# Attention scores and row maxima of a fused transformer layer as pairs of 64-row TensorE tiles

## The reference, cut to what matters

```python
B, T, D, H, dh = 2, 2048, 256, 16, 16
q, k, v = split(x @ qkv_w + qkv_b)                       # per head (B, H, T, 16)
std_logits = einsum('bhqd,bhkd->bhqk', q, k) * dh ** -0.5
write_lines = exterior(x_prev @ w1_write, x @ w2_write)  # per head 6 numbers, unit length
read_lines = exterior(x @ w1_read, x @ w2_read)
geo_logits = einsum('bqhi,bkhi->bhqk', read_lines, write_lines @ J6) * inc_scale
std_out = softmax(causal(std_logits)) @ v
geo_out = softmax(causal(geo_logits)) @ (x @ geo_w + geo_b)
combined = (1 - gate) * std_out + gate * geo_out         # gate: mean sigmoid per token
x = layernorm(x + combined @ out_w + out_b)
x = layernorm(x + ffn(x))                                # silu(x wg) * (x wu) @ wd
```

## Time and profile before

| what | value |
|---|---|
| median of 3 runs | 2105.75 us (2104.53 to 2110.35) |
| profiled execution, first to last instruction | 2112.1 us |
| TensorE busy | 1930.6 us, 91% |
| ScalarE busy | 1273.4 us, 60% |
| VectorE busy | 1129.4 us, 53% |
| GpSimd busy | 336.9 us, 16% |
| mean granted TensorE clock | 0.962 |

### The profile page before, as it was taken

How to read it: one execution, slowest core, us unless ns; L and a number is a source line. 1 busy time by engine, 2 the same in 40 slices (tenths; PEclk the granted TensorE clock), 3 DMA queues, 4 the chain that set the end, 5 groups by cost and what they waited for, 6 DMA issues and landing times. The chain is left out here.

```text
span 2112.1 us, 35917 instructions
## 1 busy us (share of the span) xinstructions
PE 1930.6 (91%) x11400; PEld 769.0 (36%) x11400; DVE 1129.4 (53%) x2179; ACT 1273.4 (60%) x1641; POOL 336.9 (16%) x609
## 2 busy tenths in 40 slices
PE   8888498999998999999899999989999995899998
PEld 4444122333332333333233333323333322556555
DVE  5666377565564655556465655646565403443442
ACT  4555544577776777677677767767777783222121
POOL 3333303111211110111111011111101111000000
PEclk9999699999999999999999999999999997999999
DMA  6668660404133250414324041432500004112000
GB/s 192 205 211 254 163 107 25 86 21 90 37 70 46 50 86 6 91 20 73 49 47 86 6 91 21 72 46 50 86 6 30 4 11 103 43 51 65 20 20 20
DMA packets 138525, 145.83 MB, mean 69 GB/s; under 512 B 46784, under 2 KB 120768, under 8 KB 136288
## 3 DMA queue, kind: packets, MB, share of 16 engines
q1 hardware_dynamic: 137136, 140.32, 30.4%
q0 software_dynamic: 624, 2.75, 0.4%
q10 hardware_dynamic: 576, 0.28, 0.1%
HBM read 88.25 MB, written 54.53 MB: 68 GB/s over the span
## 5 line engine op out<-in xcount | busy, mean ns | idle before, releaser
L931 ACT ACTIVATE prob<-ex 128x1024 f32<-128x1024 f32 (+2 forms) x1280 | 1074.5, 893 | 444.4 <-PE ex L776 438.8
L946 DVE TENSOR_REDUCE mp<-mx 128x1 f32<-128x512 f32 (+3 forms) x1280 | 749.2, 609 | 547.4 <-PE mx L794 287.5
L776 PE MATMUL ex<-qa,ka 98*128 98x512 bf16 (+3 forms) x2560 | 675.6, 354 | 62.7 <-issue 28.3
L827 PE MATMUL pv<-prob,va 128*32 128x512 f32 (+3 forms) x5120 | 613.4, 552 | 7.6 <-POOL prob L752 7.3
L791 PE MATMUL mx<-ka,qa 96*128 96x512 bf16 (+3 forms) x1280 | 450.1, 353 | 14.7 <-DVE mp L946 13.8
L752 POOL TENSOR_SCALAR_AFFINE_SELECT prob<-prob 128x256 f32<-128x256 f32 x512 | 205.8, 408 | 1288.3 <-ACT prob L931 1287.8
L776 PEld LDWEIGHTS ex<-qa,ka 98*128 98x128 bf16 x2560 | 200.2, 99 | 474.3 <-ACT prob L931 306.3
L791 PEld LDWEIGHTS mx<-ka,qa 96*128 96x128 bf16 x1280 | 123.7, 97 | 340.4 <-DVE mp L946 239.1
L827 PEld LDWEIGHTS pv<-prob,va 128*32 128x32 f32 x5120 | 101.7, 108 | 206.7 <-issue 181.8
L1291 ACT ACTIVATE sg<-pg 128x512 f32<-128x512 f32 x48 | 28.7, 597 | 185.6 <-PE pg L1213 185.5
L794 PE MATMUL mx<-mask_qk,ident 128*128 128x128 bf16 x512 | 113.1, 221 | 0.0
(11 more groups left out here) (101 smaller groups left out, 964.7 us busy)
## 6 DMA issues: line engine op xcount, KB each, us to landing
parts<-sp SPq DMA_DIRECT2D x64, 384.0 KB, 3.3
qa<-parts SPq DMA_DIRECT2D x192, 128.0 KB, 6.7
ka<-parts SPq DMA_DIRECT2D x192, 128.0 KB, 8.6
values<-vn SPq DMA_DIRECT2D x64, 256.0 KB, 3.3
va<-values SPq DMA_DIRECT2D x16, 1024.0 KB, 13.8
heads<-on SPq DMA_DIRECT2D x64, 128.0 KB, 1.9
att<-heads SPq DMA_DIRECT2D x64, 128.0 KB, 3.0
xc<-in_xt SPq DMA_DIRECT2D x8, 513.0 KB, 4.2
```

Of the source, the lines that this page charges most:

```text
L776: last = pe.matmul(dst, ka[which][0:NROWM, h, kb * P:(kb + 1) * P], qa[which][0:NROWM, h, (qt + 1) * CH - w:(qt + 1) * CH], start=True, st ...
L827: last = pe.matmul(pv[h * VW:(h + 1) * VW, qt % 2, CH - w:CH], va[kind][:, kb, h * VW:(h + 1) * VW], prob[(s * HG + h) % 8][:, at[j]:at[j] ...
L931: act.activation(prob[n % 8][:, 0:w], ex[:, n % 2, 0:w], ACT.Exp).then_inc(ex_done, 1)
L946: v.tensor_reduce(out=mp[kind][:, h * NKB + qb, k0 // CH:k0 // CH + 1], in_=mx[:, u % 2, 0:w], axis=AX.X, op=ALU.max).then_inc(mx_free[kin ...
```

## The change

- The geometric numbers are no longer padded: 6 per head. In the projection they fill 2 row tiles of 96 rows and not 4 of 128, so NR is 6, and `t32` and `d32` have a buffer for each row tile. DRAM parts are two tensors now.
- A geometric score is 6 x 6 + 2 = 38 rows. Two heads lie in one operand, at rows 0 and 64, and the two matmuls use the two 64-row halves of the array. A dot-product score keeps 98 rows (odd heads: 128, with zeroed rows between).
- A unit of a step is now two heads and one block of keys, not one head and two blocks. The exponent still reads 1024 columns in a full step, and there are still four units in a step. `times_v` of block 0 waits only for the first two units.
- The maxima use 4 of the 6 products, 64 rows, and two heads at once in the two halves; a tile is a pair of heads, 80 tiles for each group of heads, and it takes both PSUM slots, so tile u waits for tile u - 1.
- The mask matmul is gone. VectorE masks instead: an off-diagonal pair is one reduce over 2 x 512 columns, a pair on the diagonal is two `tensor_tensor_reduce` instructions that add the mask and take the maximum, with their output thrown away into `dull`.
- `spread` weighs a geometric step 1.9 times a dot-product step. It gives the DOT item 28 pair tiles (15 off, 13 on the diagonal) and the GEO item 52 (33 and 19); the first item has 80 (48 and 32). There are four places in a step: before the first scores, before `times_v` of block 0, after it, and before `times_v` of block 1.
- The two maximum rows are copied by four DMAs, not two, and GpSimd sets rows of ones and zeros for each of the two operand sets in four memsets, in the first two items.

```diff
@@ load_operands
+    n = (NCOMP, DH)[kind]
     for i in which:
-        j, side, n = i // (2 * NCOMP), (i // NCOMP) % 2, i % NCOMP
-        src = parts[side, kind, b, (Q_PARTS, K_PARTS)[side][n], bass.ds(g * (HG * DH) + j * 2 * DH, 2 * DH), :]
-        q.dma_start((q_set, k_set)[side][n * DH:(n + 1) * DH, 2 * j:2 * j + 2, :],
-                    src.rearrange("(h d) t -> d h t", h=2)).then_inc(loaded[j], 16)
+        j, a, side, piece = i // 12, (i // 6) % 2, (i // 3) % 2, i % 3
+        to = (q_set, k_set)[side]
...
+        q.dma_start(to[row:row + 2 * n, at, :], src).then_inc(loaded[j], 16)
@@ project: first_rest
-                if not (head and m < 4):
-
-                    v.wait_ge(p3_done, c * NR + m - 3)
-                v.tensor_tensor(out=d32[m % 4][:, :], in0=t32[m % 4][:, :], in1=sp3[m][:, 0, :],
+                if not head:
+
+                    v.wait_ge(p3_done, (c - 1) * NR + m + 1)
+                n = ROWS[m]
+                v.tensor_tensor(out=d32[m][0:n, :], in0=t32[m][0:n, :], in1=sp3[m][0:n, SLOTS[m][0], :],
                                 op=ALU.subtract).then_inc(d_done, 1)
@@ attend: gpsimd, aside
+                if it < 2:
+                    i = it + 1
+                    done = 3 + it * 4
+
+                    g.wait_ge(masked, (it * len(DIAGONAL) + len(DIAGONAL) - TT // 2) * UNITS)
+                    g.memset(ka[i][96:98, 0:2, :], 1.0).then_inc(ones_ready, 1)
+                    g.wait_ge(ones_ready, done + 1)
+                    g.memset(ka[i][32:64, 2:4, :], 0.0).then_inc(ones_ready, 1)
...
@@ attend: tensor, scores
-                for (kb, w), c0 in zip(blocks, at):
-                    dst = ex[:, slot, c0:c0 + w]
-                    last = pe.matmul(dst, ka[which][0:NROWM, h, kb * P:(kb + 1) * P],
-                                     qa[which][0:NROWM, h, (qt + 1) * CH - w:(qt + 1) * CH],
+                kb, w = blocks[u // 2]
+                for a in range(2):
+                    dst = ex[:, pair, a * CH:a * CH + w]
+                    if kind == GEO:
+                        rows, at = slice(HALF * a, HALF * a + GEO_FULL), pair
+                    else:
+                        rows, at = slice(0, DOT_FULL[a]), 2 * a + pair
+                    last = pe.matmul(dst, ka[which][rows, at, kb * P:(kb + 1) * P],
+                                     qa[which][rows, at, (qt + 1) * CH - w:(qt + 1) * CH],
                                      start=True, stop=True)
@@ attend: tensor, max_tile
-                if u >= 2:
-
-                    pe.wait_ge(mx_free[kind], p * (NMX * COUNT[kind]) + (u - 1) * COUNT[kind])
-                dst = mx[:, u % 2, 0:w]
-                last = pe.matmul(dst, qa[which][0:NROW, h, qb * P:(qb + 1) * P],
-                                 ka[which][0:NROW, h, k0:k0 + w], start=True, stop=not on_diagonal)
-                if on_diagonal:
-                    last = pe.matmul(dst[:, w - P:w], ident16[:, :], mask_qk[:, :], start=False, stop=True)
+                if u >= 1:
+
+                    pe.wait_ge(mx_free[kind], p * (NMX * COUNT[kind]) + u * COUNT[kind])
+                for a in range(2):
+                    n = GEO_ROWS if kind == GEO else DOT_MAIN
+                    rows, at = slice(HALF * a, HALF * a + n), pair if kind == GEO else 2 * a + pair
+                    last = pe.matmul(mx[:, a, 0:w], qa[which][rows, at, qb * P:(qb + 1) * P],
+                                     ka[which][rows, at, k0:k0 + w], start=True, stop=True)
@@ attend: vector, max_tile
-                v.tensor_reduce(out=mp[kind][:, h * NKB + qb, k0 // CH:k0 // CH + 1], in_=mx[:, u % 2, 0:w],
-                                axis=AX.X, op=ALU.max).then_inc(mx_free[kind], COUNT[kind])
+                if on_diagonal:
+                    v.sem_inc(v_passed, 1)
+                    for a in range(2):
+                        last = v.tensor_tensor_reduce(out=dull[:, a, 0:w], in0=mx[:, a, 0:w], in1=mask_qk[:, CH - w:CH],
+                                                      scale=1.0, scalar=3 * MASKED, op0=ALU.add, op1=ALU.max,
+                                                      accum_out=to[:, a:a + 1])
+                else:
+                    last = v.tensor_reduce(out=to, in_=mx[:, :, 0:w], axis=AX.X, op=ALU.max)
+                last.then_inc(mx_free[kind], COUNT[kind])
@@ attend: tensor, step
-                scores(it, which, s, 0, head)
                 some(0)
-                scores(it, which, s, 1, head)
+                scores(it, kind, which, s, 0, head)
+                scores(it, kind, which, s, 1, head)
                 some(1)
                 if has_before:
                     times_v(*before, 0, head)
                 some(2)
-                scores(it, which, s, 2, head)
+                scores(it, kind, which, s, 2, head)
+                scores(it, kind, which, s, 3, head)
                 some(3)
-                scores(it, which, s, 3, head)
-                some(4)
                 if has_before:
                     times_v(*before, 1, head)
-                some(5)
```

More of the change, by code:

```diff
@@ L80 @@
 LAST_OF = {qt: max(s for s, x in enumerate(STEPS) if x[0] == qt) for qt in range(NQT)}
[L83 to L87, removed]
 def max_tiles():
     out = []
-    for h in range(HG):
+    for pair in range(HG // 2):
         for qb in range(NKB):
@@ L96, in max_tiles @@
             for k0 in range(0, end, CH):
-                out.append((h, qb, k0, min(CH, end - k0), k0 + CH >= end))
+                out.append((pair, qb, k0, min(CH, end - k0), k0 + CH >= end))
     return out
@@ L104, with spread @@
 MT_STEP = NSTEP - 2
-def spread(steps_of):
-    size = [sum(w for _, w in STEPS[s][1]) + 2 * P if s >= 0 else 0 for s in steps_of]
-    cols = [w + (P if d else 0) for _, _, _, w, d in MAXT]
+def spread(room):
+    cost = [(2 * w + 300) if d else (2 * w + 150) for _, _, _, w, d in MAXT]
     out, u, done = [], 0, 0
-    for i in range(len(steps_of)):
+    for i in range(len(room)):
         mine = []
-        while u < NMT and done + cols[u] / 2 <= sum(cols) * sum(size[:i + 1]) / sum(size):
+        while u < NMT and done + cost[u] / 2 <= sum(cost) * sum(room[:i + 1]) / sum(room):
             mine.append(u)
-            done += cols[u]
+            done += cost[u]
             u += 1
@@ L564, in chunk @@
                 v.wait_ge(dve, base + 7)
[L565 to L568 removed]
+                if not head:
                     v.wait_ge(rows_ready, c * NR)
                 v.tensor_tensor(
[L572 removed]
+                    out=ln[:, :, 1, :, :], in0=line_v[:, :, 0, :, :],
                     in1=rn[:, :, 0, :].unsqueeze(3).to_broadcast([P, TT, H, NCOMP]),
@@ L585, in _, with attend @@
                 first_rest(NC - 1, m, False)
-def attend(nc, parts, values, heads, ident, ident16, mask_qk, wide, out_w, out_b, wg, wu, wd, weights,
-           first):
+def attend(nc, parts, values, heads, ident, mask_qk, wide, out_w, out_b, wg, wu, wd, weights, first):
     with ExitStack() as ctx:
@@ L764, in _, with scores @@
             is_wide = pe.value_load(wide[0:1, 0:1], min_val=0, max_val=1)
-            def scores(it, which, s, h, head):
-                n = s * HG + h
-                slot = n % 2
+            def scores(it, kind, which, s, u, head):
+                n = s * UNITS + u
+                pair = u % 2
                 if not (head and n < 2):
@@ L848, in step @@
                 later = list(maxima[s])
-                where = [WHERE[min(len(later), 6)].count(i) for i in range(6)]
-                where[5] += max(len(later) - 6, 0)
+                where = [WHERE[min(len(later), 4)].count(i) for i in range(4)]
+                where[3] += max(len(later) - 4, 0)
                 def some(i):
```

212 lines of the change are left out of this document (124 added, 88 removed).

## The result

The changed kernel is slower: 2338.92 us median of 4 runs (2337.09 to 2344.12) against 2108.05 us for the kernel before on the same chip, a ratio of 1.110 (95% interval 1.108 to 1.112). The forecast was 2048 us, with a range up to 2120. Medians are of fast executions; the one run that was slow, 2331.91 us in the last experiment, is left out. The profiled execution agrees: its span is 2338.1 us against 2112.1.

What follows compares the result with a forecast made beforehand. TensorE was taken to bound the attention, with ScalarE next, and VectorE to pace the projection. Projection -24, seven head groups -40 and first item +6 sum to -58, from 2105.75 to 2048 us; range 1990 to 2120.

Steps and rivals of the forecast that it cites:

- costed at nothing: Work assumed hidden: GpSimd's memsets, SyncE's wait for them, four row copies, and 24 load issues an item ahead; no added time.
- The projection, -24: Projection: VectorE's chain starts 3.07 us earlier in each of 7 chunks, -21.5, and less GpSimd work at the end, -2.9.
- the low end: Projection: if the shorter wait keeps TensorE's clock up, up to 1.6 us more a chunk, -11.
- A dot-product item, 84: Attention: 76.0 us without maxima, plus 4.9 for 28 pair tiles and 3.6 for tile-shape changes; 84 against 91.5.
- A geometric item, 95: Attention: scores halve, but TensorE's wait for VectorE to read each pair tile takes over; 95 us against 93.2.
- the cycle of 1.70: Maxima off the diagonal: 1.23 us reduce of 1024 columns, 0.05 to TensorE's start, 0.42 to the next reduce.
- While TensorE waits in these steps its clock can fall: Geometric items: TensorE's clock may drop during its wait for VectorE, adding 1.5 us an item.
- The first item, 149.5: First attention item: 80 pair tiles bound by the wait for VectorE, 125.4 us, plus other parts; 149.5 against 143.5, +6.
- the diagonal instruction is dear: Rival, VectorE's masked maxima: `tensor_tensor_reduce` costs well over a reduce, kernel slower, 2104 or 2157 us; chance 0.13.
- the halves don't run at once: Rival, TensorE's 64-row matmuls: a score pair stays 0.43, each tile's cycle grows 0.2, 2176 us; chance 0.07.
- attention gains nothing: Rival: tile-shape changes cost 0.25 or TensorE's clock falls more; only the projection's 24 stay, 2078 to 2099; chance 0.15.
- the wait hurts less: Rival: `take` and tails hide and the clock holds; geometric 88, dot-product 80, about 1970 us; chance 0.13.

Runs made afterwards that it cites:

- the last experiment: Kernel before, with VectorE's mask instead of the mask matmul, its maxima matmuls reading 64 rows and not 96: 2307.95 us, ratio 1.091.
- wide loads: Changed kernel with each operand load's outermost dimension 16 (dot product) or 6 (geometric) in place of 2: 2195.67 us, ratio 1.042.
- the short reduces: Changed kernel with operand loads of outermost dimension 16 or 6, VectorE's maxima reading 4 columns and row maxima constant at 40: 1936.16 us, ratio 0.918.
- halves: Changed kernel with operand loads of outermost dimension 16 or 6, each half of `mx` having its own semaphore and reduce: 2127.52 us, ratio 1.009.
- fewer tiles: Changed kernel with operand loads of outermost dimension 16 or 6, `GEO_SHARE` 1.0 for 1.9, so 40 pair tiles per item: 2108.18 us, ratio 1.001.

## Why the prediction was wrong, point by point

**The step that failed** is the one costed at nothing: "The loads are 24 issues as before, an item ahead, and the geometric ones smaller." The count was right; the form was not looked at. The new loads copy one block of rows twice (`to_broadcast([2, n, T])`) or take two slots, so that the outermost dimension is 2, where it was 16. While the loads run the DMA share is 0.13, and 0.96 for wide ones, and a set takes 47 us where a wide one takes 13. The Trainium skill, "DMA: Bandwidth & Descriptors", section "Rules for kernel authors", says that the slowest dimension sets how many of the 16 engines a transfer uses, and that an outermost zero-stride broadcast of c copies keeps it on at most c. The trace agrees: two of 16 is 0.125, and the window of the loads has 0.13. The loads themselves did have the time, an item ahead; but the cover asked for was that of the queue behind them, the stores. Undone, it gives 143 us back; done to the kernel before, it costs 471. These differ, so it is no fixed price. In the old kernel the geometric sets are as large as the others, and VectorE waits for the store 14 times, not 6; in the changed one the geometric sets (48 KB an issue) are out after 20 us.

**The projection, -24.** Measured -21, by two errors that met. The chunk's period and SyncE's loads show it; VectorE in the changed kernel:

```profile
137.90 0.21 DVE L550 TENSOR_TENSOR gate_z<-gz,bg 128x64 f32 x1
160.50 0.21 DVE L550 TENSOR_TENSOR gate_z<-gz,bg 128x64 f32 x1
191.68 0.21 DVE L550 TENSOR_TENSOR gate_z<-gz,bg 128x64 f32 x1
```

The period fell to 22.6 from 27.4 (104.82 to 132.17 before), 4.8 and not 3.07: the shorter wait gave more back, as the low end had it (the wait of 3.80 is 0.72, the four matmuls behind it take 1.98 for 2.69, and the clock in such a chunk is 1.00 for 0.94). But the last one is 31.2, when the first item's narrow loads share the queue with the projection's own stores, for which ScalarE waits. With wide loads it is 24.0 and the projection ends at 210.6 and not 220.6: 31 under the kernel before.

**A dot-product item, 84.** Measured 87.4, 3.4 us too much; with the short reduces it is 86.0, so 1.4 of it is the wait for VectorE and 2.0 is not taken apart. The price of a change of tile shape, 0.13, was near: 0.1.

**A geometric item, 95.** The terms hold where the clock does: 1.71 for the cycle of 1.70, 0.69 for the masked instruction, and less than the sum for two, since they overlap. The term behind "While TensorE waits in these steps its clock can fall", +1.5, was mis-sized. With wide loads, so without the stores' wait, the items take 106 and 110, 11 to 15 over the forecast, at 0.89 and 0.81. At the lower level a cycle costs 0.22 more, and the values no longer fit beside a reduce. That the wait and the low clock feed each other is how I read the rows; what the runs show is that whatever shortens the wait (halves, fewer tiles, small reduces) raises the clock too: 0.92, 0.91, 0.96 to 1.0. "Its gain is spent on the wait" was right and too mild.

**The first item, 149.5.** Measured 193, at a clock of 0.65, with wide loads still 190 (219 to 408.7) at 0.63. So here the loads are not the cause. The wait for VectorE's reduces is: with the short ones the item takes 116, at 0.86. The step that failed is the cycle of 1.70, taken at the full clock for all 80 tiles (and without the +1.5 that the geometric item got). The cycle's 0.22 on 80 tiles is 18 of the 40; the rest is not taken apart.

**The sum.** From the forecast's parts to the windows: projection +3, first item +43, seven groups (213.0 each, the mean period of the `negm` reduces, for 179) +238, last item +4: 288 of the 291 us missed. The loads are 143 of it. With them wide the period is 194.7, so the groups are 7 x (194.7 - 179) = 110 too long, the first item is 40 and the last 4, and the projection is 7 shorter than forecast: 147 of the 148 us that are left.

**The rivals.** That the diagonal instruction is dear: no, it takes 0.69 us at 512 columns and 0.489 in the mean; the forecast's price of a reduce (1.05 ns a column and 0.152) gives 0.488 for the mean width of 320. That the halves don't run at once: no, 0.39 for two. That attention gains nothing through tile shapes and clock: right in kind and named, but given 2099 at most, since it counted neither the queue nor what the clock does to a chain. That the wait hurts less: no, though 1936 us with small reduces shows what it would have been worth. (Its own terms, -117, -35 and the first item's +6, give 1960 and not the 1970 written.) The Trainium skill, "TensorEngine Tiling (Array Packing)", section "Tiling Modes", says that a change of tiling mode drains TensorE. The last run agrees, at 0.1 us a time: the next weights are loaded only when the tile's columns are through.

What stays open: how the lower clock and the wait divide the 11 to 15 us of a geometric item, since no run held the clock while it changed the wait; and where the first item's other 22 us are. A version with two pairs of `mx` slots wasn't tried.

## What to carry to other kernels

When a change touches a transfer, read the access pattern and not only the count and the bytes, then name what stands behind it on its queue. A resource that goes from two buffers to one turns everything behind the waiting instruction into its round trip (354 us on the kernel before alone), and releasing it by halves won back 68 us here. Work made smaller for TensorE is not cheaper if it changes the tile shape between its neighbours: 64 rows in place of 96 cost some 200 us.

## What was unexpected in the hardware

- Behind DMAs whose outermost dimension is 2 the issuing queue slows down: three issues of 128 KB take 7 to 8 us, six take 2.7 when it is 16.
- Matmuls of 96 and 98 rows follow each other with the weights loaded under the one before; 64 and 98 rows don't, and each such change costs 0.1 us. 38 behind 64 rows behave as one shape (the load of 957.44 above, 0.08 after the tile's matmul has begun).
- `tensor_tensor_reduce` with two inputs runs at the speed of a plain reduce, and its accumulator read of 0.08 us overlaps the next one.
- A loop of waits pays for the lower clock in each round: the tile's cycle is 1.93 us and not 1.71, eight value matmuls 1.93 and not 1.06.
